# Attention over a memory: batches of one and then two tiles, and products that follow the scores by five halves in place of six

## The chip, the cores and the metric

One NeuronCore of a Trainium2 chip runs the whole program. The time is the device time of one execution in microseconds (us). The kernel before has three timed runs and one profiled execution.

## What is computed

The reference applies three residual stages to 4096 tokens of 128 features: a mixture of eight experts, an attention of every token over a fixed memory of 4096 keys and values, and the same mixture again.

```
x = x + 0.5 * _L0_ffn_ref(_layernorm(x, axis=-1), ...)     # mixture of experts, weights shared with the third line
x = x + _L0_attn_ref(_layernorm(x, axis=-1), ...)
x = x + 0.5 * _L0_ffn_ref(_layernorm(x, axis=-1), ...)

q = hidden_states @ Wq.T + bq
scores = einsum('bshd,hmd->bshm', q, memory_keys) / sqrt(128)
probs = softmax(scores, axis=-1)
mem_out = einsum('bshm,hmd->bshd', probs, memory_values)
output = mem_out @ Wo.T + bo
```

Only `output` of the attention is returned. The matmuls of scores and of values are computed with every operand split into a high and a low part, so that each product takes three matmuls.

## The kernel before

The tokens form 8 groups of 4 tiles of 128 tokens. The attention works in **units**: unit u is group u // 2 against one half (2048) of the keys, so there are 16 units, numbered 0 to 15 (`LAST`). A unit has 8 **halves** h: tile h // 2 against 1024 of the keys. H = 8u + h counts halves through all units. Every engine runs one Python loop over u and h, and its program order is the order of these loops; semaphores (`wait_ge`) tie the engines together.

In half h of unit u:
- TensorE (PE) makes the scores (`scores`, L1244 to L1246: two banks of 512 keys, three matmuls each). It then makes one **pair** of value products (`values`, L1285 to L1287, six matmuls), and at the end of the half it transposes the next pair of its own tile's probabilities (`transpose_pair`, L1264) into one PSUM bank called `TB`.
- VectorE (DVE) takes the maximum of the scores (`maximum`, L998) and after every second half the negated maximum (L1004), turns 32x32 squares of a finished half (`transpose_squares`, L993), and makes the low part of the pair in `TB` (`own_low`, L986).
- ScalarE (ACT) makes the exponentials (`exponentials`, L670 and L680), the high part of the pair in `TB` (`own_high`, L644) and the high part of the pair that came by DMA (`moved_high`, L652).
- GpSimd (POOL) makes the low part of the latter (`moved_low`, L460).

A value product needs the probabilities with the keys on the partitions. For tile 3 of a unit PE transposes them. For tiles 0 to 2 (`MOVED = 3`; in units 0 and 15 only tiles 0 and 1) DVE turns the 32x32 squares inside tensor `E` (`E2` in the code) and DMAs then carry strips of 32 partitions to their places in `probsT`. These DMAs go in **batches**: batch 0 holds tiles 0 and 1, batch 1 holds tile 2. A batch is 16 strips. SyncE (SP) issues them once the squares of the batch's last tile are done; 4 of the 16 strips of batch 1 are issued by ACT behind half 7, and half of unit 0's strips by ACT too. A strip is 128 KB when a batch holds two tiles and 64 KB when it holds one. Semaphore `moved[k]` counts what has landed of batch k. `E` is written again by the exponentials of the next unit, so the first exponentials of a tile wait for its batch of the unit before:

```
if i < MOVED and h == 0:
    wait(act, moved[batch_of(i)], moves(batch_of(i), u))
```

`moved_high` waits for both batches before it reads the first pair of a unit.

`LAG` says how far the value products stand behind the scores: the first pair of unit w is multiplied in half LAG of unit w + 1 (unit 0 has `FIRST_LAG = 2`), and the high and low parts of it are made up to four halves earlier. The pairs of unit 15 are therefore multiplied after the last scores. The bank `TB` also serves three other matmuls: the output projection of a finished unit (`project_out`, L1295, half LAG + 1), the transposes of the next group's normalised input (L1062, half `Q_HALF` of odd units) and its projection to q (L1225, half `Q_HALF` + 1). Each of them waits for `own_low` of the pair that is in the bank, and the next pair's transposes wait until ACT or DVE has read the result out (`copy_y` L695, `copy_xT_for_q` L623, `q_high` L629, `q_low` L955). `copy_oT` (L689) reads the finished sum of value products.

DVE also has work at fixed halves: in even units the statistics of the next group in half 0, `merge_shifts` in half 1 and `merge_shares` (L972 to L979) in half 5. After the last scores the loops run on for two more units' worth of halves. There the last pairs, the first normalisations (L798), the routing of the third stage (`route_group`, L844 to L882), the spread of its weights (L813), its transpose (L1094) and its copy (`copy_wbc`, L564) are put at fixed halves that do not depend on `LAG`, while `copy_oT` of unit 15 does depend on it. Then comes `ffn(1)`, whose first matmul (L1120) waits for `copy_wbc`.

## Time and profile before

| what | value |
|---|---|
| median of 3 runs | 674.98 us (672.7 to 675.78) |
| profiled execution, its own time | 673.04 us |
| span of that execution | 671.4 us |
| mean granted clock of TensorE | 0.975 of full speed |
| PE busy | 613.3 us (91% of the span) |
| DVE, ACT, POOL busy | 530.8, 461.5, 381.9 us |

Times in the trace count from the start of the span. The first stage lasts until about 120 us, the attention until 581 us, the last stage until the end. Matmul records overlap, since the array is a pipeline, so the distance between two starts says more of a matmul's cost than its recorded length.

### The profile page before, as it was taken

The page shows a single profiled execution, that of the slowest core. Times are in us where ns is not written, and L with a number is a line of the kernel's source. Part 1 is how long each engine was busy: PE and PEld are TensorE (multiplying, and loading weights), DVE is VectorE, ACT ScalarE, POOL GpSimd, SP SyncE. Part 2 cuts the span into 40 slices and gives each one's busy share as a digit, 9 for nine tenths or more (in the row PEclk, how much of TensorE's full clock was granted, in tenths as well). Part 3 has the DMA queues.
Part 4 walks back from the last instruction along what each step waited for, and adds up shares of the span by engine and source line. Part 5 has one row for each costly group of instructions (what it writes and reads, how often), then busy time and mean ns, then how long its engine had stood idle before and what let it go on. Part 6 is the DMA issues. An engine that isn't in the chain of part 4 may idle for free.

```text
span 671.4 us, 9169 instructions
## 1 busy us (share of the span) xinstructions
PE 613.3 (91%) x2784; PEld 432.9 (64%) x2800; DVE 530.8 (79%) x968; ACT 461.5 (69%) x765; POOL 381.9 (57%) x378
## 2 busy tenths in 40 slices
PE   3888989669989999999999999999999987999997
PEld 2444434447667877778778778787787866645542
DVE  4889877858977887887897897897898765699885
ACT  3576777446667767777777786776776753577886
POOL 3856660035366766767687587586587783533100
PEclk9899999969998999999999999999999986999999
DMA  8021210043463553743734636527436320000000
GB/s 296 2 62 33 62 32 0 17 110 78 111 163 75 140 122 85 167 103 89 170 86 122 154 73 151 130 69 175 109 86 162 92 61 1 0 18 16 32 33 31
DMA packets 35555, 59.06 MB, mean 88 GB/s; under 512 B 8539, under 2 KB 9139, under 8 KB 35379
## 3 DMA queue, kind: packets, MB, share of 16 engines
q1 hardware_dynamic: 31891, 53.75, 31.8%
q10 hardware_dynamic: 3616, 4.73, 2.8%
q8 instruction: 23, 0.38, 0.3%
q14 instruction: 25, 0.20, 0.1%
HBM read 8.12 MB, written 2.10 MB: 15 GB/s over the span
## 4 chain that ended last, share of the span: by engine, by line
PE 62%; DVE 17%; issue 6%; ACT 4%; SPq 4%; POOL 3%; DMA 1%; ACTq 1%; DVEq 0%; POOLq 0%
PE banks L1244 7%; PE banks L1246 7%; PE banks L1245 7%; PE banks L1285 7%; PE banks L1286 6%; PE banks L1287 6%; PE banks L1264 4%; SPq L308 4%; PE banks L1120 4%; DVE probsT L895 3%; PE banks L1129 3%; DVE bank_max L998 3%; DVE E L993 3%; PE banks L1136 3%; PE banks L1295 2%
## 5 line engine op out<-in xcount | busy, mean ns | idle before, releaser
L460 POOL TENSOR_TENSOR p_lo<-probsT,p_hi 128x768 fp32r<-128x768 f32 (+1 forms) x128 | 226.7, 1776 | 174.7 <-ACT p_hi L652 174.5
L998 DVE TENSOR_REDUCE bank_max<-banks 128x1 f32<-128x1024 f32 x128 | 156.2, 1220 | 36.5 <-PE banks L1246 35.4
L652 ACT ACTIVATE p_hi<-probsT 128x768 fp32r<-128x768 f32 (+1 forms) x128 | 104.5, 816 | 22.9 <-PE banks L1287 18.9
L1244 PE MATMUL banks<-kv_lo,q_parts 128*128 128x512 f32 x256 | 112.6, 440 | 7.3 <-ACT E L670 4.8
L559 ACT ACTIVATE probsT<-probsT 128x1024 bf16<-128x1024 bf16 x96 | 92.2, 980 | 34.5 <-DVE probsT L895 31.6
L993 DVE STREAM_TRANSPOSE E<-E 128x1024 f32<-128x1024 f32 x92 | 113.6, 1234 | 2.1 <-ACT E L670 2.1
L895 DVE SCALAR_TENSOR_TENSOR probsT<-banks,E 128x1024 bf16<-128x1024 f32 x80 | 95.5, 1217 | 22.5 <-PE banks L1120 20.6
L1285 PE MATMUL banks<-p_hi,kv_lo 128*128 128x512 f32 x256 | 110.0, 430 | 2.5 <-POOL p_lo L460 2.1
L670 ACT ACTIVATE E<-banks,neg_max 128x1024 f32<-128x1024 f32 x92 | 102.4, 1113 | 7.4 <-DVE neg_max L1004 4.6
L644 ACT ACTIVATE p_hi<-banks 128x256 fp32r<-128x256 f32 (+1 forms) x128 | 52.3, 409 | 78.5 <-PE banks L1264 78.3
L1286 PE MATMUL banks<-p_lo,kv_hi 128*128 128x512 f32 x256 | 104.0, 406 | 0.0
L1287 PE MATMUL banks<-p_hi,kv_hi 128*128 128x512 f32 x256 | 103.7, 405 | 0.0
L1246 PE MATMUL banks<-kv_hi,q_parts 128*128 128x512 f32 x256 | 102.2, 399 | 0.0
L1245 PE MATMUL banks<-kv_hi,q_parts 128*128 128x512 f32 x256 | 101.9, 398 | 0.0
L986 DVE TENSOR_TENSOR p_lo<-banks,p_hi 128x256 fp32r<-128x256 f32 (+1 forms) x128 | 56.2, 439 | 50.4 <-ACT p_hi L644 50.2
L1264 PE MATMUL banks<-ident,probs 128*128 128x128 f32 x272 | 53.6, 281 | 9.7 <-ACT probs L680 6.6
L1285 PEld LDWEIGHTS banks<-p_hi,kv_lo 128*128 128x128 f32 x256 | 49.5, 193 | 15.4 <-issue 3.3
L1244 PEld LDWEIGHTS banks<-kv_lo,q_parts 128*128 128x128 f32 x256 | 48.9, 191 | 15.9 <-ACT E L670 6.4
L1264 PEld LDWEIGHTS banks<-ident,probs 128*128 128x128 f32 x272 | 37.6, 144 | 32.0 <-ACT probs L680 7.1
L1287 PEld LDWEIGHTS banks<-p_hi,kv_hi 128*128 128x128 f32 x256 | 49.2, 192 | 12.6
L1286 PEld LDWEIGHTS banks<-p_lo,kv_hi 128*128 128x128 f32 x256 | 49.5, 193 | 11.8 <-issue 1.7
L1120 PE MATMUL banks<-E,wup_b 128*128 128x512 bf16 x166 | 50.6, 386 | 7.0 <-ACT probsT L548 6.1
(110 smaller groups left out, 880.3 us busy)
## 6 DMA issues: line engine op xcount, KB each, us to landing
probsT<-E SPq DMA_DIRECT2D x248, 128.0 KB, 2.4
probsT<-E SPq DMA_DIRECT2D x168, 64.0 KB, 2.0
E<-in_keys_values SPq DMA_DIRECT2D x8, 512.0 KB, 3.5
probsT<-E ACTq DMA_DIRECT2D x56, 64.0 KB, 2.4
out<-X SPq DMA_DIRECT2D x8, 256.0 KB, 2.1
X<-in_x SPq DMA_DIRECT2D x1, 1280.0 KB, 9.5
probsT<-E ACTq DMA_DIRECT2D x8, 128.0 KB, 4.1
X<-in_x SPq DMA_DIRECT2D x3, 256.0 KB, 5.6
```

Source lines behind the costliest of these rows:

```text
L460: pool.tensor_tensor(moved_part(p_lo, ring), moved_pair(ring // UP, ring % UP), moved_part(p_hi, ring).bitcast(fp32), ALU.subtract).then_i ...
L652: act.activation(moved_part(p_hi, ring), moved_pair(ring // UP, ring % UP), ACT.Copy).then_inc(moved_hi_done, 1)
L895: dve.scalar_tensor_tensor(hidden[:, k, :, :], up_banks[PAIR_BANK[k]], 0.0, spread.unsqueeze(1).to_broadcast([P, 2, N]), ALU.max, ALU.mult ...
L993: dve.transpose(half, half).then_inc(squares_done, 1)
L998: dve.tensor_reduce(bank_max[:, i % 2, h:h + 1], score_pair(u, i, h).rearrange("p b n -> p (b n)"), AX.X, ALU.max).then_inc(bank_max_done, 1)
L1244: pe.matmul(bank, qh, kl, start=True, stop=False)
L1245: pe.matmul(bank, ql, kh, start=False, stop=False)
L1246: pe.matmul(bank, qh, kh, start=False, stop=True).then_inc(scores_done, 1)
L1264: last = pe.transpose(TB[:, at_column:at_column + P], own_exponentials(w, t)[:, c * P:(c + 1) * P], ident[:, :])
L1285: pe.matmul(OB, vl, hi, start=(c == 0), stop=False)
L1286: pe.matmul(OB, vh, lo, start=False, stop=False)
L1287: pe.matmul(OB, vh, hi, start=False, stop=(c == KC - 1)).then_inc(pv_done, 1)
```

## The change

The batches are cut the other way: the first holds tile 0 alone, the second tiles 1 and 2, except in units 0 and 15, which have one batch of tiles 0 and 1 as before. The first batch can be issued two halves earlier, the second has 16 strips of 128 KB in place of 64 KB, and ACT issues a quarter of them. The waits of the exponentials and of one copy are adapted. `LAG` becomes 5, and with it the half of the output projection, the half in which POOL adds a block, and `Q_HALF`, all one earlier.

```diff
-BATCHES = ((0, 2), (2, 1))
+BATCHES = ((0, 1), (1, 2))
+END_BATCHES = ((0, 2),)
...
-LAG = 6
+LAG = 5
 FIRST_LAG = 2
 PROJECT_HALF = LAG + 1
 ADD_HALF = LAG
-Q_HALF = 5
+Q_HALF = 4
...
-        def batch_of(i):
-            return [k for k, (first, count) in enumerate(BATCHES) if first <= i < first + count][0]
+        def batches(u):
+
+            return END_BATCHES if u in (0, LAST) else BATCHES
+
+        def batch_before(u, i):
+
+            return 0 if i == 0 or u < 2 else 1
...
-            first, count = BATCHES[k]
+            first, count = batches(u)[k]
...
-                for k, (first, count) in enumerate(BATCHES):
-                    if first >= moved_tiles(u):
-                        continue
+                for k, (first, count) in enumerate(batches(u)):
                     sp.wait_ge(squares_done, squares_of(u) + 2 * (first + count))
...
-                    wait(act, moved[batch_of(i)], moves(batch_of(i), u))
+                    wait(act, moved[batch_before(u, i)], moves(batch_before(u, i), u))
...
                 dve.wait_ge(weights_ready, route_event(GROUPS) + 1)
+                dve.wait_ge(moved[0], moves(0, UNITS))
```

**ACT at the start of unit 2.** Before, the rows in order are the copy of unit 0's finished sum, the exponentials of halves 0 and 1, the copy of unit 0's projection (L695), the exponentials of half 2, and then the first `moved_high` of unit 1 (L652), which waits for both batches.

```order
L689 ACTIVATE attended<-banks 128x512 [waits pv_done]
L670 ACTIVATE E,row_sum<-banks,neg_max 128x8x4x32 [waits moved0,neg_max_done]
L670 ACTIVATE E,row_sum<-banks,neg_max 128x8x4x32 [waits neg_max_done]
L695 ACTIVATE attended<-banks 128x512 [waits out_proj_done]
L700 ACTIVATE shift_exp<-shift 128x8 [waits shift_done]
L670 ACTIVATE E,row_sum<-banks,neg_max 128x8x4x32 [waits moved0,neg_max_done]
L652 ACTIVATE p_hi<-probsT 128x768 [waits pv_done,moved1,moved0]
L644 ACTIVATE p_hi<-banks 128x256 [waits pv_done,probsT_done]
```

With the change the same place reads as follows; L693 is L689 before, L699 is L695, L674 is L670, L656 is L652, L648 is L644.

```order
L693 ACTIVATE attended<-banks 128x512 [waits pv_done]
L674 ACTIVATE E,row_sum<-banks,neg_max 128x8x4x32 [waits moved0,neg_max_done]
L674 ACTIVATE E,row_sum<-banks,neg_max 128x8x4x32 [waits neg_max_done]
L656 ACTIVATE p_hi<-probsT 128x768 [waits pv_done,moved1,moved0]
L699 ACTIVATE attended<-banks 128x512 [waits out_proj_done]
L704 ACTIVATE shift_exp<-shift 128x8 [waits shift_done]
L648 ACTIVATE p_hi<-banks 128x256 [waits pv_done,probsT_done]
L674 ACTIVATE E,row_sum<-banks,neg_max 128x8x4x32 [waits moved1,neg_max_done]
```

The `moved_high` that waits for both batches now stands ahead of the projection's copy and of the exponentials of half 2.

**ACT at the end of the attention.** Before, the last rows are the high parts of the last two pairs in `TB`, the copy of the spread weights (L564), the copy of unit 15's sum (L689), and the first square of the last stage.

```order
L644 ACTIVATE p_hi<-banks 128x512 [waits pv_done,probsT_done]
L652 ACTIVATE p_hi<-probsT 128x512 [waits pv_done]
L644 ACTIVATE p_hi<-banks 128x512 [waits pv_done,probsT_done]
L564 ACTIVATE E<-banks 128x512 [waits weighted,wbc_done]
L689 ACTIVATE attended<-banks 128x512 [waits out_proj_done,pv_done]
L559 ACTIVATE probsT<-probsT 128x1024 [waits weighted]
```

With the change:

```order
L648 ACTIVATE p_hi<-banks 128x512 [waits pv_done,probsT_done]
L656 ACTIVATE p_hi<-probsT 128x512 [waits pv_done]
L648 ACTIVATE p_hi<-banks 128x512 [waits pv_done,probsT_done]
L693 ACTIVATE attended<-banks 128x512 [waits out_proj_done,pv_done]
L568 ACTIVATE E<-banks 128x512 [waits weighted,wbc_done]
L563 ACTIVATE probsT<-probsT 128x1024 [waits weighted]
```

The copy of unit 15's sum, which waits for the last value product, now stands ahead of the copy of the spread weights.

**PE after the last scores.** Before, half 7 of the first loop step behind unit 15 begins with unit 14's output projection (L1295) and a gate product (L1303), and then come the value products (L1285) of that half.

```order
L1264 MATMUL banks<-ident,E 128x128 [waits p_lo_done]
L1264 MATMUL banks<-ident,probs 128x128
L1295 MATMUL banks<-wo_s,attended 128x128 [waits oT_copied,p_lo_done]
L1295 MATMUL banks<-wo_s,attended 128x128 x3
L1303 MATMUL banks<-gate_s,probs 128x8 [waits xT_copied]
L1303 MATMUL banks<-gate_s,probs 128x8 x3
L1285 MATMUL banks<-p_hi,kv_lo 128x512 [waits moved_lo_done,p_lo_done]
```

With the change (L1300 is L1295 before, L1269 is L1264, L1290 to L1292 are L1285 to L1287, L1308 is L1303):

```order
L1300 MATMUL banks<-wo_s,attended 128x128 [waits oT_copied,p_lo_done]
L1300 MATMUL banks<-wo_s,attended 128x128 x3
L1290 MATMUL banks<-p_hi,kv_lo 128x512 [waits moved_lo_done,p_lo_done]
L1291 MATMUL banks<-p_lo,kv_hi 128x512
L1292 MATMUL banks<-p_hi,kv_hi 128x512
L1290 MATMUL banks<-p_hi,kv_lo 128x512
L1291 MATMUL banks<-p_lo,kv_hi 128x512
L1292 MATMUL banks<-p_hi,kv_hi 128x512
L1269 MATMUL banks<-ident,E 128x128 [waits p_lo_done,y_copied]
L1269 MATMUL banks<-ident,probs 128x128
L1269 MATMUL banks<-ident,E 128x128
L1269 MATMUL banks<-ident,probs 128x128
```

The projection stands one half earlier, and a pair of value products and a group of transposes now stand between it and the gate product.

## Rows read from the trace of the kernel before

**Rows 1.** The page, part 1: busy time by engine.
```profile
PE 613.3 (91%) x2784; PEld 432.9 (64%) x2800; DVE 530.8 (79%) x968; ACT 461.5 (69%) x765; POOL 381.9 (57%) x378
```

**Rows 2.** Busy time in stretches: window, length, PE, PEld, DVE, ACT, POOL, clock, DMA share, GB/s.
```profile
201.60:205.00 3.40, 3.40 (x10) 2.66 (x9) 2.46 (x5) 2.10 (x4) 3.06 (x2) 0.50 0.40 98
...
220.20:246.00 25.80, 25.44 (x122) 20.25 (x121) 22.99 (x43) 18.89 (x35) 20.55 (x18) 1.00 0.48 115
...
560.00:570.20 10.20, 9.33 (x32) 8.16 (x33) 3.49 (x11) 1.91 (x4) 1.04 (x2) 0.50 0.00 0
```

**Rows 3.** The chain through unit 8, an even unit: start, length, engine and line.
```profile
339.83 0.23 PE banks L1246
...
342.86 0.24 PE banks L1246
...
345.70 0.21 DVE part L972
...
346.50 0.34 DVE p_lo L986
...
349.12 0.32 DVE p_lo L986
...
349.49 1.16 PE banks L1295 x8
```

**Rows 4.** Strips by line L308: unit 0's, then both batches of unit 7.
```profile
L308 SPq DMA_DIRECT2D probsT<-E x8: 587/1138/1337, 131.5 to 138.7; - x8
L308 ACTq DMA_DIRECT2D probsT<-E x8: 755/1060/1187, 131.5 to 138.7; - x8
...
DMA to landing us min/median/max: 2.5/4.0/4.6
...
L308 SPq DMA_DIRECT2D probsT<-E x28: 586/597/1552, 292.7 to 311.0; - x28
...
DMA to landing us min/median/max: 2.0/2.4/3.4
```

**Rows 5.** Timeline, unit 6's last squares and ACT in unit 7's halves 1 and 2.
```profile
297.97 1.23 DVE L993 STREAM_TRANSPOSE E<-E 128x1024 f32<-128x1024 f32 x1
...
310.11 0.84 ACT L652 ACTIVATE p_hi<-probsT 128x768 fp32r<-128x768 f32 x1
...
313.14 0.84 ACT L652 ACTIVATE p_hi<-probsT 128x768 fp32r<-128x768 f32 x1
```

**Rows 6.** Timeline of unit 2 (its start to unit 3's), then unit 4's start.
```profile
167.69 1.23 DVE L993 STREAM_TRANSPOSE E<-E 128x1024 f32<-128x1024 f32 x1
...
177.12 1.05 PE L1295 MATMUL banks<-wo_s,attended 128*128 128x128 f32 x8
177.93 0.48 PE L1244 MATMUL banks<-kv_lo,q_parts 128*128 128x512 f32 x1
...
180.65 0.85 ACT L652 ACTIVATE p_hi<-probsT 128x768 fp32r<-128x768 f32 x1 [0.47 <-issue]
...
189.76 0.48 PE L1244 MATMUL banks<-kv_lo,q_parts 128*128 128x512 f32 x1
...
220.28 0.48 PE L1244 MATMUL banks<-kv_lo,q_parts 128*128 128x512 f32 x1
```

**Rows 7.** Timeline of unit 3: ACT's wait for a DMA, and PE.
```profile
199.65 1.11 ACT L670 ACTIVATE E<-banks,neg_max 128x1024 f32<-128x1024 f32 x1 [2.53 <-DMA probsT<-E]
...
200.91 0.50 PE L1244 MATMUL banks<-kv_lo,q_parts 128*128 128x512 f32 x1 [1.78 <-ACT E L670]
```

**Rows 8.** Timeline after the last scores, up to the last stage's first matmul.
```profile
560.13 0.68 DVE L986 TENSOR_TENSOR p_lo<-banks,p_hi 128x512 fp32r<-128x512 f32 x1
...
560.87 2.08 PE L1295 MATMUL banks<-wo_s,attended 128*128 128x128 f32 x8 [3.73 <-DVE p_lo L986]
...
578.51 0.59 ACT L564 ACTIVATE E<-banks 128x512 f32<-128x512 f32 x1
...
581.14 0.38 PE L1120 MATMUL banks<-E,wup_b 128*128 128x512 bf16 x1
```

## The prediction

> **What bounds the kernel now.** I read the page first: PE is busy 613.3 of 671.4 us [rows 1]. Then the busy time by stretches. In a unit in the middle of the attention PE is busy 25.44 of 25.80 us at full clock, with DVE at 22.99, ACT at 18.89 and POOL at 20.55 [rows 2]. So PE's own work sets the pace there, DVE is close behind, and ACT has 27% of its time free. The chain through an even unit shows where even there something is lost. A half takes 342.86 - 339.83 = 3.03 us, and ahead of the output projection the chain leaves PE and runs through DVE: `merge_shares` from 345.70 on, `own_low` until 346.84, another one until 349.44, and only then the projection at 349.49 [rows 3]. Last come the places outside the steady units. In unit 3 ACT waits 2.53 us for a DMA, PE waits 1.78 us for ACT [rows 7], and then the granted clock is 0.50 for 3.4 us [rows 2], the 1.2 GHz level. After the last scores PE waits 3.73 us for `own_low` [rows 8], and again the clock falls, to 0.50 for 10.2 us [rows 2]. The change touches all three: the steady units, the DMAs and the end.
>
> **What the change removes, adds and moves.** No arithmetic is added or removed. A pair of value products moves from behind the last scores to unit 2, every projection into `TB` moves one half forward, and the strips change size and time. I cost it at four places, against the profiled execution's 673.04 us.
>
> **A, the start of the attention.** In unit 2, `moved_high` of unit 1's first pair now stands ahead of the copy of unit 0's projection, and that copy frees `TB` for PE's transposes. It waits for batch 1 of unit 1, which can go when the squares are done at 167.69 + 1.23 = 168.9 [rows 6]. No row shows 12 strips of 128 KB from SP together with 4 from ACT. The nearest is unit 0: 8 and 8 of them, first issue 131.5, last 138.7, 4.0 us to landing, so 11.2 us [rows 4]. SP alone issues 28 strips of either size from 292.7 to 311.0, 0.68 us each [rows 4], so 12 of them and 2.4 us to landing would be 8.1 + 2.4 = 10.5 us. I take 11.2, since both engines issue at once here too: landed at 180.1. Then `moved_high` 0.85 [rows 6] and the copy, 0.6 us like the copy of the same size at 578.51 [rows 8]: 181.6. PE, which had projected at 177.12 and began its next scores at 177.93 [rows 6], begins them at about 181.9, 4.0 us late. Behind the copy ACT still owes one `own_high` and the exponentials of half 2, 1.8 us, so half 5 begins at 183.7, and three halves, now all with value products, end at 183.7 + 3 x 3.03 = 192.8. Unit 3 began at 189.76 [rows 6]: **+3.1 us**, of which 1.4 are the pair that has moved here.
>
> In unit 3, exponentials of half 0 wait for batch 0 of unit 2 (2.53 us, [rows 7]). With one tile in it that batch can go two halves, 6 us, sooner; the wait goes. With it go PE's 1.78 us and the cost of the clock, half of 3.40 us busy at 0.50 [rows 2], 1.7 us: **-3.5 us**. The new wait in unit 2 leaves PE without work for some 3.7 us, as long as the one after which the clock fell at 560. A drop costs 1.7 us as in unit 3, or nothing where PE waits anyway; I take **+1.0** (bounds 0 and 2).
>
> **B, the steady units.** The projection moves from half 7 to half 6. PE's last score matmul of half 5 ends at 343.10, of half 6 at 346.13, of half 7 at 349.16. So the projection waited 349.49 - 349.16 = 0.33 us; in half 6 it waits for the `own_low` that ends at 346.84, because `merge_shares` stands right ahead of it on DVE: 346.88 - 346.13 = 0.75 us [rows 3]. That is 0.4 us more in each of six even units (4 to 14), **+2.4 us**. Behind it scores, squares and strips of half 7 come later by up to 1.7 us. In odd units there is no `merge_shares`; the transposes for q move to an even half, where `own_low` comes behind a negated maximum. No row shows that wait; it is at least nothing and at most the length of the projection's, 0.33 us. I take 0.1, five times: **+0.5**. A gain isn't excluded, since DVE has 2.8 us free in such a unit [rows 2]: at most the 0.33 us of now, six times, 2.0.
>
> **C, the batches in the steady units.** `moved_high` of a unit's first pair stood at 313.14 in unit 7 and now stands where 310.11 is [rows 5]. Its last squares end at 297.97 + 1.23 = 299.2 [rows 5]. By SP's own pace batch 1 lands 10.5 us later, at 309.7; by unit 0's row 11.2 later, at 310.4 [rows 4]. So the strips gain about as much as `LAG` takes away, and there is no slack left. With B's later squares it can be 0.3 to 1.6 us late. What is late next is ACT, with the exponentials of half 2 behind it, on which PE's scores of half 5 depend; ACT is free 27% of a half, 0.8 us [rows 2], and that hides as much. In odd units the q transposes wait for the `own_low` behind it. I take 0.2 us in five odd units: **+1.0** (bounds: nothing, and 0.8 us in eleven units, 8.8). The Trainium skill, page "DMA: Bandwidth & Descriptors", section "Issuing engines are not separate DMA queues", says that DMAs started by different engines share the same 16 DMA engines, so that a second issuer saves only issue time. Unit 0's rows agree with it: the median issue there is 1138 ns on SP and 1060 ns on ACT, against 597 ns in unit 7 [rows 4]. By that rule batch 1 takes 11.2 us in each unit; by SP's pace alone the sum would be 1 us lower.
>
> **D, the end.** The wait of 3.73 us is the projection of unit 14 behind six steps of `route_group` on DVE: `own_low` runs only at 560.13 [rows 8]. One half earlier it stands ahead of the routing. That wait goes, **-3.7**, and with it the clock at 0.50, during which PE was busy 9.33 us [rows 2], half of them too much: **-4.7**. One half less is left, a pair (six matmuls, 1.4 us) and its transposes: **-1.9**. In their place: the projection waits for ACT's 0.6 us and DVE's 0.68 us [rows 8] on the pair just transposed, 1.5 us. The transposes of the next half wait behind the routing, which loses cover of only one pair, 1.3. Two later ones wait behind the weights' spread and the last block, 1.3 and 0.9, of which 0.6 was there before. And at the very end `copy_oT`, which waits for PE's last value product, now stands ahead of the copy that the last stage's first matmul needs. It was done at 578.51 + 0.59 while PE worked until 581.14 [rows 8]; now two copies of 0.6 us lie open, 1.3 with the hand-over: together **+5.7**. The clock can fall again, since PE is idle as often, only in smaller pieces; a third of the 4.7 comes back, **+1.6** (bounds 0 and 4.7). D is -3.0.
>
> **The sum.** A -0.4 + 1.0, B +2.9, C +1.0, D -3.0: +1.5 us, 674.5 us for such an execution. The median of the runs shown is 1.9 us above the profiled one, so 676.4, rounded to **676.5 us**.
>
> **The rivals.** What a measurement of this kernel tells from no change is about 0.5%, 3.4 us: 671.6 and 678.4.
> - *Faster.* The end decides: the projection is out from behind the routing, the clock stays up, and DVE's free time swallows B. Then the sum loses 1.0 (A's clock), 2.9 (B), 1.0 (C) and 1.6 (D's clock): 670 us. For it speaks the size of one wait, 3.73 us with 10.2 us of slow clock behind it; against it that `merge_shares` stands where it does. It decides if the projection's wait in even units stays below 0.4 us. Chance 0.28.
> - *Slower.* Batch 1 lands late. Place: `moved_high` behind half 1 of every unit from 2 to 15. Beyond 0.8 us late it costs what is beyond, in 11 units; at 1.4 us late 6.6 us in place of C's 1.0, so 682 us. For it speaks that four times 64 KB more per issuer run through engines that unit 0's issues already slowed to 1.1 us; against it that SP has the queue to itself most of the time. This is also the case in which the change doesn't do what it says, strips that come no sooner. Chance 0.27.
> - *No change*, the forecast: PE's work is the same and the places cancel. Chance 0.45, its own range 672 to 680.
>
> **The numbers.** Lower end: the clock, B and C cost nothing, 670, and B's waits turn into its gain of 2.0: 668. Upper end: C near its bound, 683. Below 671.6: 0.28; above 678.4: 0.27.
>
> **What would show it.** In the changed profile: in unit 2 ACT's `moved_high` (L656) at about 180 and PE's transposes idle before it; in unit 3 no DMA wait on L674; in an even unit the projection (L1300) with an idle of about 0.75 us on DVE; waits of L656 on a DMA of up to 1.6 us; L1300 near 556 with a wait of about 1.5 us, no stretch of 10 us at 0.50 near the end, and L1125, the last stage's first matmul, behind L568 with an idle of 1.3 us. The prediction is wrong if batch 1 takes more than 12 us or less than 10, or if the clock falls in stretches that PE's waits don't explain.

## The result, and the profile after

| | before | changed |
|---|---|---|
| median of 4 runs each | 674.29 us (672.7 to 675.78) | 696.32 us (691.52 to 702.47) |
| profiled execution, its own time | 673.04 us | 695.24 us |
| span | 671.4 us | 693.6 us |

The changed kernel takes 1.0311 times as long, 95% interval 1.0272 to 1.035: 21 to 22 us slower, where 676.5 was forecast and 683 was the end of the range. One of the changed kernel's four runs, 702.47 us, was a slow one: it counts in the median, but not in the ratio, and without it the median is 695.24 us.

Part 1 of the changed kernel's page, to hold against [rows 1]:

```profile
PE 617.2 (89%) x2784; PEld 433.0 (62%) x2800; DVE 534.6 (77%) x968; ACT 459.5 (66%) x765; POOL 380.5 (55%) x378
```

No engine has more work; all wait more. Where, the start of each unit tells, read as the start of its first score matmul in the timeline. Lengths of units in us, from one start to the next:

| unit | 2 | 3 | 4 | 5 | 6 | 7 | 8 | 9 | 10 | 11 | 12 | 13 | 14 | 15 to the end |
|---|---|---|---|---|---|---|---|---|---|---|---|---|---|---|
| before | 21.8 | 30.5 | 25.8 | 27.1 | 26.1 | 26.9 | 25.8 | 26.9 | 25.8 | 26.9 | 25.8 | 26.9 | 26.6 | 160.4 |
| changed | 26.8 | 28.3 | 27.2 | 27.8 | 30.3 | 27.9 | 27.1 | 28.0 | 30.2 | 27.9 | 27.2 | 27.9 | 32.8 | 155.6 |

Units 4 to 14 lose 23.6 us, 18.9 of them in the six even units, where the forecast had 3.9 for all eleven. Units 6, 10 and 14 stand out. The end gains 4.8.

The same as busy time by stretches, for units 4, 6 and 7 (columns as in [rows 2]):

```profile
223.70:250.90 27.20, 25.90 (x124) 20.21 (x121) 22.67 (x44) 18.65 (x35) 19.91 (x18) 1.00 0.48 117
278.70:309.00 30.30, 27.16 (x123) 21.45 (x121) 24.15 (x44) 18.66 (x35) 19.97 (x18) 0.94 0.42 105
309.00:336.90 27.90, 27.12 (x130) 20.90 (x127) 20.85 (x29) 19.95 (x36) 18.14 (x12) 1.00 0.46 114
```

The waits of ACT, then of PE, from 205 to 535 us (waited for: us in total, times, longest):

```profile
ACT p_hi L656 <- issue: 22.8, 12, 2.4
...
PE banks L1300 <- DVE p_lo L991: 14.9, 6, 4.8
PE banks L1067 <- DVE p_lo L991: 4.8, 6, 1.1
```

Two things are new. The first `moved_high` (L656) of every unit waits, 1.9 us on average; "issue" means that nothing in the trace released it, and the row at 321.90 below shows that it is the landing of batch 1. And in the six even units the projection (L1300) waits 14.9 us for `own_low`, where it waited 2.9 before.

**The late batch**, in the timeline: the last squares of unit 6 on DVE, ACT in unit 7, the last squares of unit 7.

```profile
308.96 1.23 DVE L998 STREAM_TRANSPOSE E<-E 128x1024 f32<-128x1024 f32 x1
...
320.04 0.21 ACT L674 ACTIVATION_READ_ACCUMULATOR E<-banks,neg_max 128x1 f32 x1
321.90 0.85 ACT L656 ACTIVATE p_hi<-probsT 128x768 fp32r<-128x768 f32 x1 [1.65 <-issue]
...
336.85 1.23 DVE L998 STREAM_TRANSPOSE E<-E 128x1024 f32<-128x1024 f32 x1
```

The strips of that batch, by line L314, from 309.5 to 321 us (durations in ns min/median/max, first and last start):

```profile
L314 SPq DMA_DIRECT2D probsT<-E x12: 592/611/1082, 310.2 to 319.0; - x12
L314 ACTq DMA_DIRECT2D probsT<-E x4: 607/754/1306, 312.4 to 314.6; - x4
...
DMA to landing us min/median/max: 2.4/3.3/4.5
```

The squares end at 308.96 + 1.23 = 310.19, the last strip lands at 321.83, `moved_high` starts at 321.90: 11.7 us. ACT had been ready since 320.25.

**The held products**, in the timeline of unit 6, POOL and then DVE and PE:

```profile
297.37 1.84 POOL L464 TENSOR_TENSOR p_lo<-probsT,p_hi 128x768 fp32r<-128x768 f32 x1 [0.31 <-ACT p_hi L656]
299.64 1.80 POOL L464 TENSOR_TENSOR p_lo<-probsT,p_hi 128x768 fp32r<-128x768 f32 x1 [0.44 <-ACT p_hi L656]
...
298.32 0.91 DVE L977 TENSOR_TENSOR part<-sums,shift_exp 128x8 f32<-128x8 f32 x1
299.26 0.16 DVE L979 TENSOR_TENSOR total<-part 128x4 f32<-128x4 f32 x1
299.46 0.18 DVE L981 RECIPROCAL inv_total<-total 128x4 f32<-128x4 f32 x1
299.67 1.79 DVE L984 TENSOR_TENSOR share<-shift_exp,inv_total 128x8 f32<-128x8 f32 x1
301.39 0.41 DVE L991 TENSOR_TENSOR p_lo<-banks,p_hi 128x256 fp32r<-128x256 f32 x1
...
301.85 1.30 PE L1300 MATMUL banks<-wo_s,attended 128*128 128x128 f32 x8 [3.13 <-DVE p_lo L991]
```

`part` and `share` are the two products of `merge_shares`, with two operands in SBUF each. `share`, 8 numbers a partition, takes 1.79 us, where its shortest in this trace is 0.17. It starts 0.03 us after one of POOL's `moved_low` and ends at 301.46, with it (301.44). `part` ends at 299.23, with the one before it (299.21). `own_low` stands behind, the projection waits 3.13 us, and after it the granted clock is 0.55, close to the 1.2 GHz level (windows):

```profile
302.40:305.70 3.30, 3.30 (x13) 2.62 (x12) 1.68 (x2) 0.60 (x1) 0.00 (x0) 0.55 0.09 23
```

In units 4, 8 and 12 only `part` is held (0.92 to 1.05 us), and the projection waits 1.25. In units 6 and 10 `share` is held too, and it waits 3.13; in unit 14 `part` and the sum behind it are, 1.76 and 1.72 us, and it waits 4.82. Units 6 and 10 are some 3.1 us longer than unit 8: 1.9 us are the longer wait, and the rest is less than the 1.5 us that 3.3 us of work at 0.55 of the clock would cost (an estimate from the row above). The Trainium skill, page "SBUF — State Buffer", section "SBUF: two separate sides", has this as a rule: DVE and GpSimd share one pair of ports as an exclusive lock, which a DVE operation with two SBUF inputs needs against a GpSimd operation that reads SBUF, and the loser waits for the whole instruction. The traces agree also in what isn't held: `own_low` has one of its two inputs in PSUM and takes 0.38 to 0.43 us beside POOL as without it. The reciprocal has one input; here it never runs beside POOL, but in unit 12 of e13 below it begins 0.12 us after a `moved_low` and takes the same 0.18 us.

### The profile page after: what moved, and what is told of

Read it like the earlier page. It is cut to its first block, busy times and chain, and to the rows that moved or that the text cites. A ratio compares the mean times of both kernels' runs of the same rounds, so it can differ in the third digit from the quotient of the medians.

```text
span 693.6 us, 9170 instructions
## 1 busy us (share of the span) xinstructions
PE 617.2 (89%) x2784; PEld 433.0 (62%) x2800; DVE 534.6 (77%) x968; ACT 459.5 (66%) x765; POOL 380.5 (55%) x378
## 4 chain that ended last, share of the span: by engine, by line
PE 34%; DVE 24%; SPq 16%; issue 12%; ACT 6%; POOL 3%; DMA 2%; ACTq 1%; DVEq 0%; POOLq 0%
SPq L314 16%; DVE bank_max L1003 5%; DVE E L998 5%; PE banks L1125 4%; PE banks L1134 3%; DVE probsT L900 3%; PE banks L1249 3%; PE banks L1251 3%; PE banks L1250 3%; PE banks L1141 2%; PE banks L1300 2%; PE banks L1290 2%; DVE p_lo L991 2%; PE banks L1291 2%; PE banks L1292 2%
## 5 line engine op out<-in xcount | busy, mean ns | idle before, releaser
L1003 DVE TENSOR_REDUCE bank_max<-banks 128x1 f32<-128x1024 f32 x128 | 156.0, 1219 | 30.2 <-PE banks L1251 29.7
L656 ACT ACTIVATE p_hi<-probsT 128x768 fp32r<-128x768 f32 (+1 forms) x128 | 104.5, 817 | 55.0 <-issue 29.0
L900 DVE SCALAR_TENSOR_TENSOR probsT<-banks,E 128x1024 bf16<-128x1024 f32 x80 | 95.5, 1217 | 25.2 <-PE banks L1125 23.4
L1290 PE MATMUL banks<-p_hi,kv_lo 128*128 128x512 f32 x256 | 109.4, 427 | 2.7 <-POOL p_lo L464 2.6
L674 ACT ACTIVATE E<-banks,neg_max 128x1024 f32<-128x1024 f32 x92 | 102.4, 1113 | 5.1 <-DVE neg_max L1009 5.1
L1292 PE MATMUL banks<-p_hi,kv_hi 128*128 128x512 f32 x256 | 103.4, 404 | 0.0
L648 ACT ACTIVATE p_hi<-banks 128x256 fp32r<-128x256 f32 (+1 forms) x128 | 52.1, 407 | 68.7 <-PE banks L1269 68.4
L1269 PE MATMUL banks<-ident,probs 128*128 128x128 f32 x272 | 52.9, 278 | 12.1 <-ACT probs L684 6.7
L1290 PEld LDWEIGHTS banks<-p_hi,kv_lo 128*128 128x128 f32 x256 | 49.1, 192 | 16.1 <-issue 6.0
L1269 PEld LDWEIGHTS banks<-ident,probs 128*128 128x128 f32 x272 | 37.5, 143 | 33.5 <-ACT probs L684 7.1
L1292 PEld LDWEIGHTS banks<-p_hi,kv_hi 128*128 128x128 f32 x256 | 49.0, 191 | 12.6
L1251 PEld LDWEIGHTS banks<-kv_hi,q_parts 128*128 128x128 f32 x256 | 49.1, 192 | 11.7
```

What stands on the lines that cost most here:

```text
L656: act.activation(moved_part(p_hi, ring), moved_pair(ring // UP, ring % UP), ACT.Copy).then_inc(moved_hi_done, 1)
L900: dve.scalar_tensor_tensor(hidden[:, k, :, :], up_banks[PAIR_BANK[k]], 0.0, spread.unsqueeze(1).to_broadcast([P, 2, N]), ALU.max, ALU.mult ...
L1003: dve.tensor_reduce(bank_max[:, i % 2, h:h + 1], score_pair(u, i, h).rearrange("p b n -> p (b n)"), AX.X, ALU.max).then_inc(bank_max_done, 1)
L1251: pe.matmul(bank, qh, kh, start=False, stop=True).then_inc(scores_done, 1)
L1290: pe.matmul(OB, vl, hi, start=(c == 0), stop=False)
L1292: pe.matmul(OB, vh, hi, start=False, stop=(c == KC - 1)).then_inc(pv_done, 1)
```

## The experiments

Each stands beside runs of the kernel before on the same chip; ratios are to those.

### Which half of the change

**e1**, the batches alone: the changed kernel with

```diff
-LAG = 5
+LAG = 6
-Q_HALF = 4
+Q_HALF = 5
```

> The changed kernel with LAG = 6 and Q_HALF = 5 again, so that only the batches differ from the kernel before. Theory 1 (late batch: every unit from 2 on pays because the first moved_high waits 1.5 to 2.1 us for the strips of batch 1): with one half more (3.03 us) between squares and moved_high that wait is gone, and so is the loss; 674 us, within 0.5% of before. Theory 2 (DVE's queue: in even units merge_shares stands ahead of the own_low that the projection waits for, and is held up further by POOL): in the old place that order is harmless too, so this theory also gives 674. A third possibility, that strips of 128 KB for batch 1 disturb the steady units by themselves, would leave 680 or more.

676.83 us, 1.0046 (1.0012 to 1.008). Units 4 to 14 take 294.5 us in place of 290.7 (read in an execution of 680 us, 3 above the median). The batches alone cost some 3 us and gain little: ACT still waits 1.7 us for a DMA in unit 3, 2.5 before. The projection waits 0.75 us in each even unit, 4.5 in all in place of 2.9. Why the batches alone cost anything wasn't taken apart.

**e2**, `LAG` alone: the kernel before with

```diff
-LAG = 6
+LAG = 5
-Q_HALF = 5
+Q_HALF = 4
```

> The kernel before with LAG = 5 and Q_HALF = 4, the batches of two and then one tile kept. In the kernel before SP issues the last 12 strips of batch 1 of unit 6 until 311.5 and moved_high follows at 313.1; one half earlier it would stand near 310.1 and wait 3 us in place of the 1.5 to 2.1 us of the changed kernel. Theory 1 (late batch): slower than the changed kernel by about 1 us in each of 11 to 14 units, 705 to 712 us. Theory 2 (merge_shares ahead of own_low, held by POOL): about the same as the changed kernel, 690 to 700, with waits of the projection on own_low in even units as large as there.

713.05 us, 1.0577 (1.0522 to 1.0632). `LAG` needs the new batches, which take 17 of its 39 us away. The time is 1 us above the 705 to 712 foretold from the late batch; but units 4, 6, 10 and 12 have a `share` of 1.79 to 1.81 us (units 6 and 10 take 32.9 and 32.8), so the other theory isn't out.

### Late batch or DVE's queue

**e3**: the changed kernel with

```diff
-                    if 2 <= u and u % 2 == 0 and h == 5:
+                    if 2 <= u and u % 2 == 0 and h == 3:
                         merge_shares(g - 1)
```

> The changed kernel with merge_shares on DVE behind half 3 of an even unit in place of half 5; nothing else. Theory 2 (DVE's queue, merge_shares ahead of own_low): the projection's waits on own_low in even units, 14.9 us in six units, fall to under 3 us, and the even units return to within 1 us of their length before; of the 18.9 us that six even units lost, 12 to 17 come back: 680 to 684 us. Theory 1 (late batch): the waits for the strips are untouched, so the time stays at 693 to 697.

690.36 us, 1.0242 (1.0186 to 1.0298), between the theories. The projection's waits fell from 14.9 to 2.7 us, but PE's transposes now wait 9.0 us for `own_low`, up to 3.3: the hold has moved with the products (`share` is 1.81 us in unit 4, 1.65 in unit 8, 1.80 in unit 12).

**e4**: the changed kernel with half the bytes in batch 1. The number of DMAs is the same; in units 3 to 14 the strips leave out tile 2's data, so its value products work on old numbers.

```diff
             first, count = batches(u)[k]
+            count = 1 if k == 1 and u > 2 else count
```

> The changed kernel with the strips of batch 1 carrying one tile in place of two in units 3 to 14, the same number of DMAs; the data of tile 2 is left out, so its value products use old numbers. With 0.64 us for each of 12 issues on SP, as for the smaller strips before, and 2.3 us to landing, the batch lands 10 us after its squares in place of 11.6. Theory 1 (late batch): the waits of moved_high for DMAs go from 1.5 to 2.1 us to below 0.4, and nearly all the loss in the steady units with them: 676 to 680 us. Theory 2 (DVE's queue): the odd units gain 1 us each, the even units keep their waits for own_low: 687 to 692.

675.97 us, 1.0046 (1.0023 to 1.0069). The strips and their landing in unit 6, by line:

```profile
L315 SPq DMA_DIRECT2D probsT<-E x12: 507/592/1524, 304.0 to 311.8; - x12
L315 ACTq DMA_DIRECT2D probsT<-E x4: 515/616/683, 306.1 to 308.0; - x4
...
DMA to landing us min/median/max: 2.0/2.1/3.4
```

```profile
313.91 0.85 ACT L657 ACTIVATE p_hi<-probsT 128x768 fp32r<-128x768 f32 x1 [0.34 <-issue]
```

`moved_high` is 10.0 us behind the squares (303.94) in place of 11.7, and 20.3 us come back. Even units up to 12 take 26.45 us, unit 14 27.0, odd ones 27.05: the long units are gone. I read this as the late batch being the whole cause. It wasn't: without the lateness ACT, POOL and DVE stand differently to each other, and `merge_shares` hardly meets a `moved_low` any more (`share` 0.17 us everywhere, `part` 0.36 to 0.55), so this run took away the lateness and most of the hold.

### Taking the wait's followers away, and the products

**e5**: the changed kernel; ACT makes a unit's first `moved_high` behind the next half's exponentials.

```diff
                         exponentials(u, h // 2, h % 2)
+                    if ring is not None and ring % UP == 0 and ring:
+                        moved_high(ring)
...
                     ring = pair_at(H + 4)
-                    if ring is not None:
+                    if ring is not None and (ring % UP or ring == 0):
                         moved_high(ring)
```

> The changed kernel, complete, with ACT's first moved_high of units 1 to 15 (the one that waits for both batches) behind the exponentials of the next half in place of ahead of them. Late batch, as the run with half the bytes suggests: the strips still land 11.6 us after the squares, but ACT has by then made the exponentials that PE's scores wait for, so the wait loses its followers; units of 26.5 and 27.1 us as with half the bytes, 674 to 680 us. Rival, that moved_high itself is what PE waits for: moved_low of POOL and the first value product come later by the two operations put ahead, some 1.5 us in each of 14 units, and the time stays at 690 or above.

684.58 us, 1.0181 (1.0148 to 1.0214). The wait for the landing is gone from ACT, units 4 to 13 are 26.8 to 27.4 us; unit 14 stays at 33.3, with a wait of the projection of 5.6 us (`part` and `share` 1.52 us each). The total is between the two expectations. With the exponentials ahead of it, the late landing costs little; but `share` is 0.17 us in units 4 to 12 here too, so this run doesn't part the two causes either.

**e6**: the changed kernel; the products and the sum of `merge_shares` on POOL.

```diff
+            def merge_totals(g):
+                pool.wait_ge(shift_exp_done, g + 1)
+                pool.tensor_tensor(part[:, :, :], sums[:, :, :], shift_exp[:, :, :], ALU.mult).then_inc(merge_b, 1)
...
-                        merge_shares(g - 1)
+                        merge_inverse(g - 1)
```

> The changed kernel, complete, with two products and the sum of merge_shares done by POOL (the first two behind half 3's work, the share ahead of the block's addition); only the reciprocal stays on DVE. Theory of exclusion (a DVE product of two SBUF operands doesn't end while POOL's moved_low runs: share took 1.79 us in place of 0.17 exactly where POOL ran until its end): the units of 30.3, 30.2 and 32.8 us go to about 27, and the project waits of 14.9 us to below 6; 680 to 686 us. Rival, only the place in DVE's queue matters, as when merge_shares stood behind half 3: 690.

688.71 us, 1.0243 (1.0211 to 1.0274). Units 6 and 10 went to 27.5 and 27.2 us as expected, unit 14 only to 31.6. The projection still waits 10.5 us: DVE's reciprocal, ahead of `own_low`, now waits for POOL by semaphore, since POOL takes up `total` only between two `moved_low`. The edit changed the kind of wait more than its size.

**e8**, both edits together:

> The changed kernel with both edits, the first moved_high behind the exponentials and the products of merge_shares on POOL. Late batch and exclusion together: even units at about 26, odd units at about 27, the end as in the changed kernel: 668 to 673 us, 1 to 4 us below the kernel before. If the two edits remove the same loss, it equals the better of the two alone, 674 to 680.

684.36 us, 1.0171 (1.0137 to 1.0204): as e5 alone. What e6 removes, e5 has removed already; unit 14 stays long (31.8 us).

### The end of the attention

**e7**: the kernel before; the routing's first steps behind the projection's `own_low`.

```diff
-                    if u == LAST + 1 and h >= 6:
-                        for k in range(6 * (h - 6), 6 * (h - 5)):
+                    if u == LAST + 1 and h == 7:
+                        for k in range(0, 8):
                             route_group(k, GROUPS)
                     if u == LAST + 2 and h == 0:
-                        for k in range(12, STEPS + 1):
+                        for k in range(8, STEPS + 1):
```

> The kernel before with nothing changed but the routing's first 12 steps: none in half 6 of the first unit behind the last scores, eight in half 7 behind own_low and eight in the next half. Theory of the end (the projection of unit 14 waited 3.73 us behind six routing steps, and the clock fell to 0.50 behind it): the wait and the 4.7 us of slow clock go, as they went in the changed kernel whose end is 6.5 us shorter: 665 to 669 us. Rival, the gain there was the one half less of LAG and the routing only moves its own lateness on to the weights' transposes: 672 to 676.

672.49 us, 0.999 (0.9967 to 1.0014). The projection's wait fell from 3.73 to 1.41 us, but transposes 12 us later wait 3.05 us for an `own_low` that now stands behind the routing, and the clock is at 0.50 for two stretches of 3.4 us in place of 10.2 in one. My theory fell; the 4.8 us that the changed kernel gains at the end come with the half less, not with the place of the routing alone.

**e12**: e7 with the products on POOL as in e6, in the kernel before.

> The kernel before, complete, with batches and LAG untouched, the products of merge_shares on POOL and the routing's first steps behind own_low. Exclusion theory: the projection's waits of 2.9 us in six even units go, and with the 1.0 us of the later routing that is 670 us, faster by 0.4 to 0.6%. Rival: POOL's three small operations delay moved_low and give it back, 672 to 674.

672.7 us, 0.9989 (0.9964 to 1.0013): no change. Before, `part` took 0.28 to 0.65 us and `share` 0.17 in units 4 to 14, and nothing was to be had from them.

### Who issues the strips

**e9**: the changed kernel; ACT's four strips of batch 1 go to SP.

```diff
-                    for b in range(QUADS // 2 if u == 0 else QUADS - k):
+                    for b in range(QUADS // 2 if u == 0 else QUADS):
...
-                    if 0 < u < LAST and h == HALVES - 1:
...
-                            move_strip(act, u, 1, QUADS - 1, i)
```

> The changed kernel, complete, with all 16 strips of batch 1 issued by SP and none by ACT. Late batch, with full price (each microsecond that the batch lands later costs a microsecond in each of some 14 units): SP alone issued strips of this size in 0.64 us each before, so 16 take 10.3 us and land 12.6 to 13 us after the squares, 1 to 1.4 us later than the 11.6 now, against 2.6 us of ACT's time saved: 705 to 715 us. Rival, that ACT's own issues are what makes it late: without them SP is faster and ACT freer, 685 to 692.

725.02 us, 1.0765 (1.0723 to 1.0808). The strips of unit 6, and ACT's row behind them:

```profile
L314 SPq DMA_DIRECT2D probsT<-E x16: 596/598/632, 322.5 to 332.1; - x16
...
DMA to landing us min/median/max: 2.4/2.4/2.5
```

```profile
334.64 0.85 ACT L656 ACTIVATE p_hi<-probsT 128x768 fp32r<-128x768 f32 x1 [2.53 <-issue]
```

The squares ended at 322.44, so the latency is 12.2 us, 0.5 more than with four strips on ACT, and 29 us are lost. The lateness was as expected, the price was far above, and lateness is only a part of it. Unit 6's batch has the shortest latency; from the squares to `moved_high` it is 12.2 to 13.5 us in units 4 to 14, 12.7 on average. The five odd units lose 5.2 us, the six even ones 20.9: `share` is held in all of units 4 to 12 (1.77 to 1.81 us), in three more than in the changed kernel, and behind the projection's waits of 3.12 us the clock is at 0.50 for 3.4 to 6.8 us each time:

```profile
312.00:318.80 6.80, 5.82 (x19) 4.94 (x20) 3.51 (x5) 1.31 (x3) 0.57 (x1) 0.50 0.08 20
```

**e10**: eight strips by ACT.

```diff
-                    for b in range(QUADS // 2 if u == 0 else QUADS - k):
+                    for b in range(QUADS // 2 if u == 0 else QUADS - 2 * k):
...
-                        for i in range(QUADS):
-                            move_strip(act, u, 1, QUADS - 1, i)
+                        for b in range(QUADS - 2, QUADS):
+                            for i in range(QUADS):
+                                move_strip(act, u, 1, b, i)
```

> The changed kernel, complete, with 8 of the 16 strips of batch 1 issued by ACT in place of 4. If the two issuers are independent, SP's 8 strips are out 6.2 us after the squares and ACT's 8 after 2.2 + 8 x 0.7 = 7.8, and the batch lands some 10 us after its squares, in time: 680 us, less what 2.6 us more of ACT's time cost. If both feed the same engines and only share their rate (16 strips in 9.4 us now, 0.59 each, against 0.64 by SP alone), it lands no sooner than 11 us and ACT is busier: 697 to 710.

743.47 us, 1.1036 (1.0987 to 1.1085). Unit 6's strips:

```profile
L314 SPq DMA_DIRECT2D probsT<-E x8: 596/612/1425, 326.3 to 331.7; - x8
L314 ACTq DMA_DIRECT2D probsT<-E x8: 593/720/1002, 328.5 to 334.2; - x8
...
DMA to landing us min/median/max: 2.5/3.4/4.2
```

Squares at 326.32, last landing at 337.46: 11.2 us. So for unit 6's batch 16, 12 and 8 strips on SP give 12.2, 11.7 and 11.2 us; each four strips that leave SP save 0.5 us of its 2.4 to 2.6. By the rule that the prediction cited, the Trainium skill, page "DMA: Bandwidth & Descriptors", section "Issuing engines are not separate DMA queues", a second issuer saves only issue time; the trace agrees that it saves little, and shows the price: with both issuing, landing takes 3.3 to 3.4 us at the median, with SP alone 2.4. ACT's issues, 6.3 us in one go, cost more than they save: ACT computes nothing for 4.91 us of it, the exponentials come later, and `moved_high` no longer waits for the batch at all, but for ACT. No `share` is held in this run, so the hold has little part in its price.

### What is left without the lateness

**e11**: e4 with e6's products on POOL.

> The run with half the bytes (the data of tile 2 left out in units 3 to 14) and the products of merge_shares on POOL together. There the even units were 26.45 us, 0.65 longer than before, the projection waited 6.8 us in six units. If it is merge_shares ahead of own_low that is left of the loss (term B of the prediction, sized at 0.4 us in an even unit), the even units go to 25.8 to 26.0 and the time 3 to 4 us below that run's: 672 to 673. If not, 676.

676.18 us, 1.0039 (1.0018 to 1.006), as e4. As in e6 the reciprocal waits for POOL, and the projection still waits 6.8 us in six units. It tells nothing of term B.

**e13**: e4 with `merge_shares` one half earlier.

```diff
-                    if 2 <= u and u % 2 == 0 and h == 5:
+                    if 2 <= u and u % 2 == 0 and h == 4:
```

> The run with half the bytes (the data of tile 2 left out in units 3 to 14) with merge_shares on DVE behind half 4 in place of half 5. If merge_shares ahead of the own_low for which the projection waits is what is left of the loss, the projection's waits of 6.8 us in six units fall below 3, the even units go from 26.45 to 25.8 to 26.0 and the time to 672 or 673. If it only moves to the transposes of the half before, as it did behind half 3, 676.

692.76 us, 1.0284 (1.0247 to 1.0322): 17 us slower than e4, by moving four small operations one half. By tile, over six units (ns min/median/max), and POOL and DVE in unit 8:

```profile
L985 DVE TENSOR_TENSOR share<-shift_exp,inv_total x6: 1490/1688/1828, 244.0 to 524.3; 128x8 f32<-128x8 f32 x6
```

```profile
351.37 3.65 POOL L465 TENSOR_TENSOR p_lo<-probsT,p_hi 128x768 fp32r<-128x768 f32 x2
355.27 1.80 POOL L465 TENSOR_TENSOR p_lo<-probsT,p_hi 128x768 fp32r<-128x768 f32 x1 [0.26 <-ACT p_hi L657]
...
353.37 1.67 DVE L978 TENSOR_TENSOR part<-sums,shift_exp 128x8 f32<-128x8 f32 x1
...
355.48 1.61 DVE L985 TENSOR_TENSOR share<-shift_exp,inv_total 128x8 f32<-128x8 f32 x1
```

Here both products fall into a `moved_low` in units 4 to 12, and `share` in unit 14. This shows the hold as a cause of its own, with the batch in time: 2 to 4.6 us for an even unit, whose length is 28.6 to 31.1 us, while the odd units stay at 27.1.

**e14**: the complete changed kernel with batch 1 split.

```diff
                 for k, (first, count) in enumerate(batches(u)):
+                    if k == 1:
+                        sp.wait_ge(squares_done, squares_of(u) + 4)
+                        for b in range(QUADS // 2):
+                            for i in range(QUADS):
+                                move_strip(sp, u, 1, b, i, (1, 1))
```

> The changed kernel, complete: half of tile 1's strips of batch 1 (8 of 64 KB) go out on SP as soon as tile 1's squares are done, in the 5 us in which SP waits for tile 2's; then the 8 of tile 2 at 64 KB, 4 of both tiles at 128 KB, and ACT's 4 as before. Closed loop (a unit lasts at least the batch's latency plus 16.2 us in odd and 18.5 us in even units): latency between that of 64 KB strips, 9.9 us, and the 11.6 us now, about 10.4, so that the odd loop is 26.6 us, under PE's 27.0, and the even one closes near PE's own length: 676 to 679 us with nothing left out. If the loss came from the bytes that all strips together move, and not from the time to the last landing, the 8 more DMAs per unit make it worse: 696 or more.

682.64 us, 1.0127 (1.0089 to 1.0165), where 676 to 679 was expected. From the squares to `moved_high` it is 10.1 us for unit 6's batch, but up to 12.1 for others; 14 us come back with every byte moved and eight more DMAs a unit. So the bytes as such aren't the loss. Units 6 and 14 are still 30 us, with `share` held (1.80 and 1.49 us); unit 10, where it is free here, takes 26.5.

**e15**: e14 with `merge_shares` behind half 4.

> The complete kernel of the split batch with merge_shares behind half 4 as well. Both causes together: 672 to 675, that is within 0.3% of the kernel before. If merge_shares only moves its wait, the same as the split batch alone.

686.22 us, 1.0202 (1.014 to 1.0263), far from the 672 to 675 expected. `part` is 1.62 to 1.85 us in four of six units, and the six even units are 3.2 us longer than in e14, but the five odd ones 3.4 us shorter. The intervals of the two overlap: that this place costs here too isn't shown by the time.

**e16, e17, e18**: `merge_shares` behind half 6, in e4, in e14 and in the changed kernel itself. POOL's addition of a block, which needs `share`, goes one half later with it; no run has that part alone.

```diff
-ADD_HALF = LAG
+ADD_HALF = LAG + 1
...
-                    if 2 <= u and u % 2 == 0 and h == 5:
+                    if 2 <= u and u % 2 == 0 and h == 6:
```

> The run with half the bytes (the data of tile 2 left out in units 3 to 14) with merge_shares behind half 6 and POOL's addition of the block one half later. If merge_shares right ahead of the projection's own_low is what was left of the loss, the projection's waits of 6.8 us in six units fall below 3 and the time to 672 to 674 from 676.0. If the hold by POOL only shows at the transposes of half 7, beyond the 1.4 us of value products that cover it, 676 to 680.

669.69 us, 0.9947 (0.9923 to 0.9971): below the kernel before, though with tile 2's data left out. The projection waits 0.7 us in six units in place of 6.8; even units take 25.35 us, 0.4 less than before the change.

> The complete kernel of the split batch (682.6 us) with merge_shares behind half 6 and POOL's addition one half later. Its projection waited 10.7 us in six even units, up to 3.4. If the place cures that: 674 to 677. If not: 682.

677.66 us, 1.006 (1.0037 to 1.0084). Even units 25.4, but odd ones 28.4 to 29.1: with the units shorter, the split batch comes too late again (`moved_high`, here L663, waits 23.4 us for strips, up to 3.2). SP's strips of unit 6:

```profile
L316 SPq DMA_DIRECT2D probsT<-E x36: 560/591/830, 288.1 to 311.0; - x36
```

SP issues all 36 strips of the unit without a pause, 23 us long, from the squares of tile 0 at 288.06. Those of tile 2 end at 301.28, after 13.2 us, and SP is still busy with earlier strips; `moved_high` follows 12.2 us behind them. In e14 unit 6 was 30.0 us long and left SP the time. The split saves bytes at the end, but in a short even unit the eight issues more stand ahead of the last ones.

> The changed kernel (696.3 us), batches untouched, with merge_shares behind half 6 and POOL's addition one half later. Of its loss, by the lengths of the units, about 12 us are units in which merge_shares was held and the projection with it (6, 10 and 14), 7 us are the late batch alone, 0.7 to 0.9 us a unit. If that split is right: 683 to 686. If the hold only moves: 692 or more.

679.04 us, 1.0093 (1.0057 to 1.0128): better than the 683 to 686 expected. Some 16 of the 21 to 22 us are back by the place of `merge_shares` (and POOL's addition), and the even units are 25.4 to 25.9 us, unit 14 26.9. PE's waits there, 205 to 535 us:

```profile
PE banks L1067 <- DVE p_lo L991: 5.1, 6, 1.9
PE banks L1300 <- DVE p_lo L991: 0.9, 1, 0.9
```

None of the complete kernels beats the kernel before.

### The four corners

| median, us | batch 1 late (all bytes) | in time (half the bytes) |
|---|---|---|
| `merge_shares` behind half 5 | 696.3 | 676.0 |
| behind half 6 | 679.0 | 669.7 |

The late batch alone costs 679.0 - 669.7 = 9.3 us; `merge_shares` ahead of the projection's `own_low` alone costs 676.0 - 669.7 = 6.3 us; both together 26.6, 11.0 more than their sum. The corners weren't all measured on one chip; each against its own kernel before, with 695.24 us for the changed one, the three are 9.3, 5.6 and 24.6 us, so the excess is 10 to 11 us. Units 6, 10 and 14 of the changed kernel, in which the lateness puts the products under a `moved_low`, are together some 12 us longer than its units 4, 8 and 12. e16 is 3.6 us below the kernel before (3.9 by the traces): 4.3 by the end and 2.6 by units 4 to 14, less 3.0 lost until unit 4.

For an odd unit the lateness can be followed as a loop. From the last squares of unit 6 to `moved_high`, and from there to the last squares of unit 7, in us:

| | to `moved_high` | on to the squares | sum | unit 7 |
|---|---|---|---|---|
| changed | 11.7 | 16.2 | 27.9 | 27.9 |
| e9, all by SP | 12.2 | 16.2 | 28.4 | 28.4 |
| e18 | 11.6 | 16.2 | 27.8 | 27.8 |
| e4, half the bytes | 10.0 | 17.1 | 27.0 | 27.0 |

That the two add up to the unit holds for any pair of points in it; what tells is that the way back is the same 16.2 us in all three kernels with the batch late, whatever the latency. Where it is in time, PE's work sets the unit, and the way back has slack. In the even units of the changed kernel the way back is 15.4 to 15.5 us in units 4, 8 and 12, 18.5 and 18.6 in units 6 and 10, where `share` is held, and 21.0 in unit 14; in e18 it is 13.9 to 14.1 up to unit 12. So `merge_shares` ahead of `own_low` stands on this way, and with a late batch, which leaves no slack, the unit pays for all of it: this is why the two losses are more together than each alone.

## Why the prediction was wrong, step by step

- **A, the start.** The mechanism was right: `moved_high` at 181.49, batch 1 landed at 181.41 where 180.1 was said, the copy, then PE's transposes after 4.15 us idle (3.7 said). Unit 2 is 5.0 us longer, where unit 3 was to begin 3.1 us later and the clock was to cost 1.0 (it is at 0.50 for 3.4 us from 183.3); unit 3 has no wait for a DMA any more and is 2.2 us shorter, 3.5 was said. With unit 2 beginning 0.6 us later, unit 4 begins 3.4 us later, where 0.6 was forecast.
- **B, the steady units: this step failed.** "That is 0.4 us more in each of six even units" let `merge_shares` keep the durations that it had, though it now meets POOL at another point of its work. The projection waits 1.25 us with `part` held, 3.13 with `share` held too, 4.82 in unit 14. Term B was 2.4 us for the even units, against the kernel before. With the batch in time they lose 3.3 us (e4, `part` 0.36 to 0.55 us): there the size was nearly right. In the changed kernel they lose 18.9, and with `merge_shares` out of the way they lose nothing, although the batch is late (e18: 0.9 us shorter than before). So it failed twice: the products were taken as long as ever, and B and C were added as if the one didn't change the price of the other. (Measured by another yardstick, the place behind half 5 against that behind half 6, B is 6.3 us in time and 16 to 17 us late.) My bounds had no row for a held product: in [rows 3] the products are short, and nothing had asked why `part` took 0.28 us in one unit and 0.65 in another.
- **C, the batches: place and landing right, price wrong.** Batch 1 took 11.6 us, 11.2 was taken (the 28 strips of [rows 4] are unit 6's, not unit 7's, which changes nothing in the sum); `moved_high` waits in every unit, and this was the place named for the case "slower". Two parts of the step failed. ACT was ready 10.1 us behind the squares in unit 7, where 10.9 had been read from before, so the lateness was 1.5 to 2.4 us and not 0.3 to 1.6. And that ACT's free time, 0.8 us a half, "hides as much" isn't so: free time elsewhere in a half doesn't shorten a loop. The term was 1.0 us, it measured 9.3 alone (e18 against e16), 4.3 of it in the five odd units, which are 0.9 us longer where 0.2 was taken. The price of the case "slower", what is beyond 0.8 us in 11 units, would give 13 us at 2 us late, more than the lateness alone cost; even so it would end at 689, and the rest is B under a late batch.
- **D, the end.** Forecast -3.0 us, measured -4.8. The projection waits 1.41 us for 1.5, the clock stays at 1.00, and the last stage's first matmul waits 1.55 us for the 1.3 said. The slow clock that was priced at 1.6 us didn't come. A stretch by windows, and that matmul in the timeline:

```profile
580.00:590.00 10.00, 7.97 (x49) 6.43 (x48) 6.78 (x15) 3.99 (x9) 5.15 (x6) 1.00 0.00 0
```

```profile
603.06 0.38 PE L1125 MATMUL banks<-E,wup_b 128*128 128x512 bf16 x1 [1.55 <-issue]
```

- What was named as making the prediction wrong, a batch 1 of "more than 12 us or less than 10", watched the one number of the step that was right. What caught the failure was the expected idle of 0.75 us ahead of the projection.

What stays open: what the batches alone cost (e1), what part of the gain of e16 to e18 is POOL's addition, and how much of unit 14's extra is the normalisation that POOL makes there (its `moved_low` come in a row of three, 5.36 us). None of these was run.

## What to carry to other kernels

A wait that closes a loop from one iteration to the next is paid in each, once latency and way back together are longer than the iteration's own work; free time of the engines on the way doesn't hide it, so add up latency and way back and hold the sum against the iteration. Before a small DVE operation with two SBUF inputs is put ahead of something that is waited for, look at what POOL runs at that time: with the batch in time (tile 2's data left out) the same four operations behind half 6, 5 and 4 made it 669.7, 676.0 and 692.8 us. And when one experiment gives nearly all back, run the other factor too: e4 looked like a full explanation, and only the four corners showed that two losses had been removed at once.

## What the runs showed of the hardware that I had not expected

- DVE products of 8 numbers a partition took up to 1.85 us (e15) while POOL's `moved_low` read SBUF, ending with POOL's operation to within 0.03 us; 0.12 to 0.19 us is what they take otherwise.
- A strip costs its issuer 0.60 us at 128 KB (e9, median 598 ns) and about as much at 64 KB (592 ns). With 16 strips by SP (e9), issuing is 10.3 of the 12.2 us; halving the bytes of the changed kernel's batch saved 1.7 us of 11.7 (e4).
- With two engines issuing strips of 128 KB at once, landing took 3.3 to 3.4 us at the median, with one 2.4 (the changed kernel, e10, e9). At 64 KB it took 2.1 us even with two (e4).
